# Token rows transposed by tile height, their casts placed before the last hidden tiles' parts, and key chunks of 400, 400, 400 and 402 columns

## What is computed

```python
x = x + xattn(layernorm(x), ctx, mask)   # 16 heads of 32; 1601 keys and values per batch
x = x + (q @ n.T) @ n                    # n = layernorm(x), q = n @ W_q.T, no softmax
x = x + moe(layernorm(x))                # 8 experts, 512 -> 2048 -> 512, top 2, softmax gate
```

## Time and profile before

| | |
|---|---|
| median of 3 runs | 1305.56 us (1305.45 to 1305.67) |
| the profiled execution, its own time | 1304.27 us |
| its span, first to last instruction | 1302.5 us |
| granted TensorE clock, mean | 0.984 of 2.4 GHz |
| PE busy / DVE / ACT / POOL | 96% / 65% / 52% / 12% of the span |
| attention, about | 0 to 920 us of the span |
| layer norms, second step, gate, places | about 920 to 975 us |
| experts | about 975 to 1291 us |

### The profile page before, as it was taken

How to read it: one execution, slowest core, us unless ns; L and a number is a source line. 1 busy time by engine, 2 the same in 40 slices (tenths; PEclk the granted TensorE clock), 3 DMA queues, 4 the chain that set the end, 5 groups by cost and what they waited for, 6 DMA issues and landing times.

```text
span 1302.5 us, 22157 instructions
## 1 busy us (share of the span) xinstructions
PE 1256.4 (96%) x8497; PEld 1170.1 (90%) x8497; DVE 840.5 (65%) x2183; ACT 675.3 (52%) x1194; POOL 156.9 (12%) x86
## 2 busy tenths in 40 slices
PE   6999999999999999999999999998779999999997
PEld 5799999999999999999999999997667988888986
DVE  4556656666566565656656556665756777877776
ACT  5345545534644454563554455345334667677673
POOL 2003101300400310130040021001040000000012
PEclk9999999999999999999999999999878999999999
DMA  7002200300220220031022013004216667676763
GB/s 286 27 1 90 79 2 15 126 28 1 90 79 2 86 83 1 2 114 53 2 90 79 1 32 121 1 1 154 85 40 231 219 227 258 226 242 238 233 213 109
DMA packets 61507, 129.05 MB, mean 99 GB/s; under 512 B 3572, under 2 KB 21120, under 8 KB 61160
## 3 DMA queue, kind: packets, MB, share of 16 engines
q1 hardware_dynamic: 59240, 120.85, 26.9%
q0 software_dynamic: 2176, 6.95, 1.6%
HBM read 121.89 MB, written 15.34 MB: 105 GB/s over the span
## 4 chain that ended last, share of the span: by engine, by line
PE 93%; DVE 3%; ACT 1%; DMA 1%; issue 1%; POOL 0%; SPq 0%; DVEq 0%; POOLq 0%
PE ptp L814 24%; PE work L814 21%; PE work L1090 8%; PE pv L929 7%; PE ptp L916 7%; PE work L852 6%; PE work L1092 4%; PE ptp L1111 2%; PE ptp L1112 2%; PE ptp L1114 2%; PE ptp L1113 2%; PE ptp L1115 2%; PE work L821 1%; DMA raw<-in_ctxT 1%; PE ptp L821 1%; DVE pt L1299 1%
## 5 line engine op out<-in xcount | busy, mean ns | idle before, releaser
L814 PE MATMUL ptp<-vw_hi,cx_hi 128*128 128x256 f32 x832 | 241.7, 291 | 0.0
L814 PE MATMUL ptp<-vw_lo,cx_hi 128*128 128x256 f32 x832 | 235.1, 283 | 0.0
L814 PE MATMUL ptp<-vw_hi,cx_lo 128*128 128x256 f32 x832 | 235.0, 282 | 0.0
L495 POOL TENSOR_TENSOR cx_lo<-raw,cx_hi 128x1664 fp32r<-128x1664 f32 x30 | 113.9, 3795 | 675.1 <-ACT cx_hi L555 675.1
L814 PE MATMUL work<-cx_hi,kw_hi 128*128 128x402 f32 x504 | 175.4, 348 | 1.7 <-POOL cx_lo L495 1.7
L814 PE MATMUL work<-cx_lo,kw_hi 128*128 128x402 f32 x504 | 174.5, 346 | 0.0
L814 PEld LDWEIGHTS ptp<-vw_hi,cx_hi 128*128 128x128 f32 x832 | 159.0, 191 | 16.9 <-issue 16.9
L814 PE MATMUL work<-cx_hi,kw_lo 128*128 128x402 f32 x504 | 173.8, 345 | 0.0
L1245 DVE SCALAR_TENSOR_TENSOR kk_lo<-work,biasT,kk_hi 128x402 fp32r<-128x402 f32 x128 | 79.6, 634 | 131.9 <-ACT kk_hi L568 131.4
L1299 DVE TENSOR_TENSOR pt<-ptp,pt 128x512 fp32r<-128x512 f32 (+1 forms) x224 | 141.5, 650 | 34.6 <-ACT pt L555 30.9
L814 PEld LDWEIGHTS ptp<-vw_lo,cx_hi 128*128 128x128 f32 x832 | 159.1, 191 | 0.0
(11 more groups left out here) (251 smaller groups left out, 2384.5 us busy)
## 6 DMA issues: line engine op xcount, KB each, us to landing
w1raw<-in_w SPq DMA_DIRECT2D x32, 1024.0 KB, 5.1
w2raw<-in_w SPq DMA_DIRECT2D x32, 1024.0 KB, 6.7
raw<-in_ctxT SPq DMA_DIRECT2D x31, 832.0 KB, 6.1
pr<-in_mask SPq DMA_DIRECT2D x8, 800.5 KB, 4.4
xrow<-x_rows SPq DMA_DIRECT2D x7, 256.0 KB, 6.0
y_rows<-y_out_rows POOLq DMA_DIRECT2D x7, 256.0 KB, 2.3
xin<-in_x SPq DMA_DIRECT2D x1, 1024.0 KB, 9.3
qwraw<-in_qwT SPq DMA_DIRECT2D x1, 1024.0 KB, 11.6
```

Source lines behind the costliest of these rows:

```text
L495: pool.tensor_tensor(cx[1][:, :, sl], raw[:, k % 2], cx[0][:, :, sl].bitcast(F32), ALU.subtract).then_inc(c_lo, 1)
L814: last = pe.matmul(dst, lhs(i, c), rhs(j, c), start=(c == 0 and (i, j) == (0, 0)), stop=(c == n - 1 and (i, j) == (1, 0)))
```

## The change

It does three things. Key chunks become 400 columns for chunks 0 to 2 and 402 for chunk 3, and `LKP` becomes 1602; `keys(k)` and `wide(bank, k)` give the slices in all places that used `k * KC`. `turn_tokens` transposes the four 128-row tiles first and the four 64-row tiles after them; each bank is signalled at its last 64-row tile. `gathered(n + 1)` moves, on ACT and on DVE, from the end of `expert` to phase 3, behind the copy or sum of hidden tile 3 and ahead of the high or low parts of tiles 2 and 3.

```diff
-KC = 402
+KC = 400
 NKC = 4
-LKP = KC * NKC
+LKP = LK + LK % 2
...
+def keys(k):
+
+    return slice(KC * k, KC * (k + 1) if k < NKC - 1 else LKP)
+
+
+def wide(bank, k):
+
+    return bank[:, 0:keys(k).stop - KC * k]
...
                     for f in range(FC):
                         low_part(p, f)
+                        if f == FC - 1 and p == NP - 1 and not last:
+                            gathered(n + 1)
                         if f:
                             hidden_hi(p, f - 1)
                     hidden_hi(p, FC - 1)
...
-                if not last:
-                    gathered(n + 1)
...
-                products(bank[:, 0:KC], lambda i, c: kw[i][:, c, (2 * h + m) * P:(2 * h + m + 1) * P],
-                         lambda i, c: cx[i][:, c, k * KC:(k + 1) * KC]).then_inc(w_full, 1)
+                products(wide(bank, k), lambda i, c: kw[i][:, c, (2 * h + m) * P:(2 * h + m + 1) * P],
+                         lambda i, c: cx[i][:, c, keys(k)]).then_inc(w_full, 1)
...
-                for c in range(C):
-                    dst, cols = yb[2 + c // 2][:, (c % 2) * SLOTS:(c % 2 + 1) * SLOTS], slice(c * P, (c + 1) * P)
-                    pe.transpose(dst[:, 0:P], xrow[:, 0, cols], ident[:])
-                    last = pe.transpose(dst[:, P:SLOTS], xrow[0:TAIL, 1, cols], ident[0:TAIL, 0:TAIL])
-                    if c % 2:
-                        last.then_inc(xg_full, 1)
+                for st, rows in ((0, P), (1, TAIL)):
+                    for c in range(C):
+                        dst = yb[2 + c // 2][:, (c % 2) * SLOTS + st * P:(c % 2) * SLOTS + st * P + rows]
+                        last = pe.transpose(dst, xrow[0:rows, st, c * P:(c + 1) * P], ident[0:rows, 0:rows])
+                        if st and c % 2:
+                            last.then_inc(xg_full, 1)
...
                     for f in range(FC):
                         summed_up(p, f)
+                        if f == FC - 1 and p == NP - 1 and not last:
+                            gathered(n + 1)
                         if f:
                             hidden_lo(p, f - 1)
                     hidden_lo(p, FC - 1)
...
-                if not last:
-                    gathered(n + 1)
```

More of the change, by code:

```diff
@@ L567, in key_hi @@
                 k, m = j // 2, j % 2
-                act.activation(kk[0][:, m, k * KC:(k + 1) * KC], work[bank][:, 0:KC], ACT.Identity,
+                act.activation(kk[0][:, m, keys(k)], wide(work[bank], k), ACT.Identity,
                                bias=biasT[:, C + 2 * h + m:C + 2 * h + m + 1]).then_inc(kv_hi, 1)
@@ L851, in score_pair @@
                         rows = slice(2 * HD * rt, 2 * HD * (rt + 1))
-                        ins = pe.matmul(work[bank_of(last, both[rt])][:, 0:KC], qbd[i][rows, cc, :],
-                                        kk[j][rows, cc, k * KC:(k + 1) * KC], start=(i, j) == (0, 0), stop=(i, j) == (1, 0))
+                        ins = pe.matmul(wide(work[bank_of(last, both[rt])], k), qbd[i][rows, cc, :],
+                                        kk[j][rows, cc, keys(k)], start=(i, j) == (0, 0), stop=(i, j) == (1, 0))
                         if (i, j) == (1, 0):
@@ L1242, in key_lo @@
                 k, m = j // 2, j % 2
-                sl = slice(k * KC, (k + 1) * KC)
+                sl = keys(k)
                 col = C + 2 * h + m
-                dve.scalar_tensor_tensor(out=kk[1][:, m, sl], in0=work[bank][:, 0:KC],
+                dve.scalar_tensor_tensor(out=kk[1][:, m, sl], in0=wide(work[bank], k),
                                          scalar=biasT[:, col:col + 1], in1=kk[0][:, m, sl].bitcast(F32),
@@ L1282, in item @@
                     own(dve, w_full, count(b, last, step))
-                    sl = slice(k * KC, (k + 1) * KC)
-                    dve.tensor_tensor_reduce(pr[:, a % 4, sl], bank[:, 0:KC], negmask[:, sl], SCALE, LOWEST,
+                    sl = keys(k)
+                    dve.tensor_tensor_reduce(pr[:, a % 4, sl], wide(bank, k), negmask[:, sl], SCALE, LOWEST,
                                              ALU.add, ALU.max, smx[:, a, k:k + 1]).then_inc(w_free, 1)
```

## The result

The changed kernel takes 1297.53 us (median of 6 runs, 1296.98 to 1299.9), the one before 1306.05 us in the same rounds. The ratio is 0.9936, with a 95% interval of 0.9925 to 0.9947: 8.5 us less, where 10.1 were forecast (1295.5). The profiled execution took 1298.87 us at a span of 1297.1 us.

The account below looks back on a forecast made before the run. PE, busy 96% of the span, was taken as the bound. Keys 4.3, transposes 5.2 and casts 0.6 us sum to 10.1 us less, from the median of 1305.56 to 1295.5 us; range 1293.0 to 1300.7.

Parts of the forecast that it names:

- Rival (a): Key chunks: two columns save only their time per column, 1.2 us; total gain 7.0, time 1298.6 us; chance 0.25.
- Part 1, the keys: Attention's key and score matmuls: two columns fewer save 3 ns in each of 1,440 slots, 4.3 us.
- so it is the count and not the start: Key matmuls: 402 columns cost 3.2 ns too many through their count, since chunk 0, starting at 0, is as slow.
- the prediction's own sign: Key spacing after the change: 400-column matmuls about 180.5 ns apart, chunk 3 still 183.8; 183 would mean two columns' time only.
- Part 2, the transposes: Experts' transposes: the new order takes 1.05 us to the hidden matmul in place of 1.79, seven times, 5.2 us.
- 0.108, as for 128 rows: Experts' transposes: 64-row ones in a row stand 0.108 us apart, as 128-row ones do; high end 0.20.
- Rival (b): Transposes give little: 64-row ones 0.20 us apart or the xg wait takes over; time 1298 to 1300.7 us; chance 0.13.
- Part 3, the casts: Change of expert: xg casts end 0.87 us sooner, which wins 0.1 us six times, 0.6 us; bounds 0 to 0.6.
- alone it could not: Change of expert: with shorter transposes only, xg comes 0.74 us late and PE gives the gain back in six of seven.
- so the wait no longer costs anything: Change of expert: PE's weight load still leads its hidden matmul by 0.13 us, so the wait's 0.1 us is won.
- The slower rival: Attention: uneven chunks expose a load at the head of every key item, 10.2 us lost, time 1308.8 us; chance 0.02.
- the rival of no gain: Experts: DVE, ACT or the weights' transfers set the pace, and two columns save only their own time; 1304 us; chance 0.05.

Follow-up runs that it names:

- e3: The kernel before with only the new key chunks of 400, 400, 400 and 402 columns; ratio to before 0.9985.
- e9: The changed kernel with 64 unused bytes ahead of the context tiles cx, moving cx and all behind it; 1285.81 us in one execution.
- e1: The kernel before with only the new order of transposes in turn_tokens; ratio to before 0.9996.
- e8: The changed kernel with the casts of xg behind hidden tile 1 in place of tile 3; 1297.43 us, ratio to before 0.9940.
- e7: The changed kernel with key chunks of 400, 402, 400 and 400 columns, starting at 0, 400, 802 and 1202; 1297.44 us in one execution.
- e10: The changed kernel with the xg casts behind hidden tile 1 and key chunks of 400, 402, 400 and 400; 1295.33 us, ratio to before 0.9928.

## Why the prediction was right or wrong

**The sum.** Forecast 10.1 us less (4.3 + 5.2 + 0.6), measured 8.5 by the medians, inside the range of 1293.0 to 1300.7. Rival (a), with 7.0, lies as near as the forecast. The parts say more than the sum.

**Part 1, the keys, is the term that was mis-sized:** 4.3 us forecast, about 2 measured (attention -1.86 and the opening; e3 2.1). The step that failed is "so it is the count and not the start", and with it the 3 ns on 1,440 slots. The drop came, 3.3 ns where 3 were taken, but on the 768 matmuls of two chunks only: 2.5 us by that, less 0.5 that the value matmuls gave back (0.03 in each of 16 half batches). By the prediction's own sign chunks 0 and 1 followed the forecast (180.5) and chunk 2 rival (a) (183). The 288 score slots, a fifth of the term, gained nearly nothing (5.20 to 5.19 us a half batch). The argument rested on chunk 0, whose columns start at 0 in their tile and were as slow as the others. But the tile itself does not start at 0 in memory, and e9, which moved it by 64 bytes, made chunk 1 slow. Rival (a), two columns are worth two columns, came near in time for a wrong reason. The straight line between 256 and 512 columns, from which the 3.2 ns of excess came, was no safe ruler either: its lower end, the value matmuls, changes with the place of the tiles too.

The gap of N/2.4 + 2.5 ns that the Trainium skill gives ("TensorE: Matmul & The Clock Gate", back-to-back issue gap), there for a single isolated matmul, fits none of these rows, where each matmul has a load of its own: the spacing was 12.5 to 17.0 ns over the columns in keys and for 256-column values 13.0 before and 7.8 in e9 (means of 119.7 and 114.5).

**Part 2, the transposes:** 0.74 us a block forecast, 0.87 measured, 6.1 us in seven. The step "0.108, as for 128 rows", which rested on the 0.13 us that a load takes, was too careful: 64-row tiles in a row stand 0.06 us apart after a first 0.11, and their loads overlap each other. That is 0.09 us; the other 0.05 is the step to the hidden matmul, 0.15 in place of 0.20. Rival (b) is out. The rule of the Trainium skill behind it, that a load overlaps a running matmul only when the row groups differ (same page, packing small matmuls), does not hold here: in the new order the loads of 128-row tiles run ahead of each other's matmuls on the same rows.

**Part 3, the casts:** they end 0.84 us sooner, 0.87 forecast. That they were needed is shown by e1: "alone it could not" holds to the tenth, with 0.71 us of waiting in the profile. What failed is "so the wait no longer costs anything": part 2 gave 0.13 us more than thought, which is just the lead that was left to the load, and so the 0.6 us did not come. e8 collects it.

**The experts together:** 5.8 us forecast, 5.77 measured. That it fits so well is luck: 0.9 us more came off the transposes, 0.6 less off the wait, and PE did not get all of the rest (0.85 in place of 0.87 us for each of six experts and 0.70 for the first).

**The slower rival and the rival of no gain** did not come: the key items begin 0.11 to 0.12 us after the last value matmul in all traces, as before. "Matmuls elsewhere change their pace" is the prediction's own sign of being wrong; the value matmuls did so by 0.2 ns (119.7 to 119.9).

## What to carry to other kernels

When two chains meet at one start, compare them before pricing an edit on either: here 0.13 us between a cast's end and a weight load said that shortening PE's chain alone would be taken back by the wait. It was worth 0.74 us of the 6.1 that it took off that chain, all at the one change of expert that had room, and the two edits together gave six times the sum of the two alone. A load that starts together with its matmul, where its neighbours lead by one, is how a wait that "costs nothing yet" looks in a trace. It can have another cause: here a change of tile height leaves the same mark, at the hidden matmul at 1121.80 too, where no cast was awaited. Before tuning the column counts of matmuls, try where their two operands lie: 64 unused bytes took more off than the whole change did, in the one execution timed.

## What was not expected of the hardware

- The pace of a matmul with the same columns depends on where its operands lie in a partition. Moving the context tiles, and all behind them, by 64 bytes took value matmuls from 119.9 to 114.5 ns, 11.8 us in the attention stage by its 16 half batches (16 x 0.74), and the one execution of the whole kernel took 1285.81 us. Moving vw and cx together by the same 64 bytes brought none of this (119.6 ns). The Trainium skill says that loading the next weights does not steal read bandwidth from a running matmul, since PE reads both by ports of their own ("TensorE: Matmul & The Clock Gate", what happens when you issue a matmul); a pace that hangs on the places of both operands is hard to fit to that. The rule behind it stays open: the table of key chunks above follows no single alignment that I tried to read into it, and the two items of one chunk can differ (180.4 and 187.0 in e7, and again in e10) with the same moving columns and other weights.
- e9's gap was not tried together with e8 and e10, nor timed in several rounds. It is the first thing to do next.
- Loads of 64-row tiles follow each other at 0.06 us, those of 128-row tiles at 0.108, though each takes 0.14 us; the matmuls between them have 64 and 128 moving columns, and no run separates the rows from the columns. At a change of tile height the load is not taken ahead, 0.09 us each way in the new order (0.20 and 0.15 us in place of 0.11 and 0.06).
- The stretch between attention and experts varies by 3.5 us between traces (135.62 to 139.12), with a mean granted clock of 0.89 in the shortest and 0.85 in the longest, which is more than the key chunks are worth.
